# The rounded half of the first 20 weight splits, moved from GpSimd to ScalarE

## Chip, cores and metric

The kernel runs on one core of one Trainium2 chip. The metric is the device time of one execution in microseconds (us). A core has five engines with a queue each, and every queue is worked off in its written order: TensorE (PE in the profile, PEld its weight loads), VectorE (DVE), ScalarE (ACT), GpSimd (POOL) and SyncE (SP), which issues all the transfers. Engines wait for each other by semaphores only.

## What is computed

The reference puts a batch of 8 sequences of 256 tokens with 512 features (2048 tokens) through four layers, each with weights of its own and conditioned on a vector per sequence:

```python
x = _L0_cond_ref(x, pos_BxS, cond_2048, ...)   # norm, attention (8 heads, rope), gated MLP 512-2048-512
x = _L1_cond_ref(x, cond_2048, ...)            # norm, attention (16 heads, unit q and k), MLP with gelu
x = _L2_cond_ref(x, cond_2048, ...)            # norm, attention with a latent k/v and a sparse mask
x = _L3_cond_ref(x, cond_2048, ...)            # experts (64-256-64), norm, silu, projection
```

All of it is float32. A product with a weight is made from split operands: a number is the sum of its rounded half (hi, in the type fp32r, which TensorE reads fast) and the difference (lo), and the kernel adds the products hi*hi, hi*lo and lo*hi.

## The kernel before

The 2048 tokens are four blocks `n` of 512 tokens. The work is planned as one list of steps (`plan.steps`): each chain of steps (a norm, a projection, a head's softmax) has its places in a table of numbers, and the list is sorted by them. `Weights.spread` puts the handling of weights between those steps. Every engine's function then walks through this one list and takes out of it what is its own, so the order on each engine is that of the list. An engine that waits at one step holds back all its later steps.

A weight piece has 128 x 512 numbers. There are 119 that are split. A piece goes three ways, in steps of the list:

- `load`: SyncE brings the piece into one of two staging buffers, `ST`. The load of piece i waits for the end of the split of piece i - 2, since they share a buffer.
- `split`: GpSimd makes the rounded half (a `tensor_scalar`, here called hi-i, L375 in the profile) and then the difference (a `tensor_tensor`, here lo-i, L378), both into one of the eight slots of `W`. The rounded half waits for the load, for the last reader of what stood in the slot (`left`, a matmul on TensorE) and for the store of it (`written`).
- `store`: SyncE writes both halves to `kept` in DRAM; a later use of the piece is a `fetch` from there.

The pieces are numbered here by `weights.order`. Pieces 0 to 4 belong to the first projections (q and k/v), 5 to 8 are the output weights `o` of layer 0, 9 to 16 and 21 on are those of its MLP (`gate` and `up`), 17 to 20 are `down`.

Around the change, ScalarE has these steps: `nsqr` (squares of x, T<-X), `nhi` (rounded half of a normalized tile, HA<-FB or HM<-FB), `raw` and `kvraw` (a projection's result out of PSUM, FB<-B), `exp` (SS<-B), `copy` of the turned probabilities (PT<-B), `cx` (CX<-B) and `act` (FB<-B). The step `cond` is two small activations, each behind a load of an activation table. VectorE has `nfin` (the normalized tile, FB<-X), `nlo` (the difference that goes with `nhi`, HA<-FB,HA) and `nsq` (the sums of the squares, T<-T). TensorE's steps that matter are `out` (CX times `o`, 12 matmuls for each of four tiles), `nvar` (few,T) and `up` (HM,W). The bank in PSUM that `out` number 2 writes is freed by `exp` 18.

In the list the splits of pieces 0 to 4 stand ahead of the first `nhi`. Around the outputs of block 0 the list reads, with what is on other engines left out:

```
out 0, split 13, out 1, split 14, exp 18, out 2, out 3, split 15, split 16, exp 19, cond, copy 16, nsqr
```

(In this line `split 13` to `split 16` are the pieces by `weights.order`.) The slot of piece 13 holds the weights that `out 0` reads, that of piece 14 those of `out 1`, and so on.

Of the kernel before, what the change touches and what calls it, by code (L numbers as in the profile page):

```python
# [10 lines left out]
ACT = mybir.ActivationFunctionType  # L11
ALU = mybir.AluOpType
# [10 lines left out]
PIECES = 123  # L23
WSLOTS = 8
STAGES = 2
FBUFS = 7
VBUFS = 3
AHEAD = 2
# [937 lines left out]
def program(nc, xT, pos, condT, biasd, cols, consts, tab2, wpack, adaw, out):  # L966
    ctx = ExitStack()
    with ctx:
# [3 lines left out]
        def tally(name, step=1):  # L972
            return Tally(ctx.enter_context(nc.semaphore(name)), step)

        X = sb("X", [128, 4, TOK])
        W = sb("W", [128, WSLOTS, 2, 512], F32R)
        ST = sb("ST", [128, STAGES, 512])
# [40 lines left out]
        def col(name, i=0):  # L1018
# [4 lines left out]
        weights = Weights(plan.steps)  # L1023
# [4 lines left out]
        s_st = [tally(f"s_st{k}", 16) for k in range(STAGES)]  # L1028
# [11 lines left out]
        a_sq, a_aff, a_nhi = tally("a_sq"), tally("a_aff"), tally("a_nhi")  # L1040
        a_sin, a_cos, a_raw, a_qsq, a_wide = (tally(x) for x in ("a_sin", "a_cos", "a_raw", "a_qsq", "a_wide"))
        a_v, a_vraw, a_ck, a_exp, a_pt, a_cx = (tally(x) for x in ("a_v", "a_vraw", "a_ck", "a_exp", "a_pt", "a_cx"))
        a_act, a_ghi = tally("a_act"), tally("a_ghi")
        a_gelu, a_y = tally("a_gelu"), tally("a_y")
# [9 lines left out]
        d_tg, d_xl = tally("d_tg"), tally("d_xl")  # L1054

        g_const, g_whi, g_wlo, g_rstd = (tally(x) for x in ("g_const", "g_whi", "g_wlo", "g_rstd"))
        g_cos, g_qlo, g_qr, g_norm, g_xb = (tally(x) for x in ("g_cos", "g_qlo", "g_qr", "g_norm", "g_xb"))

        tallies = [
            s_const, *s_x0, s_x, s_pos, s_tab, s_out, *s_st, s_ad, s_cv, s_ct, s_id, s_rot, s_swap, p_adt, d_ad, *s_w, p_ada, p_tot, p_var, p_bc, p_qkv, p_rot, p_ss,  # L1060
            p_nb, p_sc, p_tr, p_va, p_out, p_up, p_down, p_first, p_second, p_last, a_silu, a_sm, a_sq,
            a_aff, a_nhi, a_sin, a_cos, a_raw, a_qsq, a_wide, a_v, a_vraw, a_ck, a_exp, a_pt, a_cx, a_act, a_ghi, a_gelu,
            a_y, d_ada, d_sm, d_gb, d_sum, d_sub, d_sq, d_var, d_nmul, d_nlo, d_trig,
            d_swap, d_sin, d_qk, d_qhi, d_khi, d_klo, d_qmax, d_ck, d_max, d_neg, d_rec, d_pt, d_cx, d_xo, d_gate, d_glo,
            d_xd, d_tg, d_xl, g_const, g_whi, g_wlo, g_rstd, g_cos, g_qlo, g_qr, g_norm, g_xb]
# [95 lines left out]
        def left(w):  # L1161

            y = weights.before[w]
            tl, key = wused[y] if y >= 0 else (p_ada, (-1,))
            return tl.of(*key)

        def written(w):

            return s_w[weights.slot(w)].of("store", weights.before[w])
# [582 lines left out]
        def scalar(e):  # L1752
# [4 lines left out]
            for step in weights.steps:  # L1757
                kind, a = step[0], step[1:]
                if kind == "cond":
                    e.wait_ge(*s_ct.of())  # L1760
                    e.activation(CT[:, 1, :, :], CT[:, 0, :, :], ACT.Silu).then_inc(*a_silu.up())
                    e.wait_ge(*d_sm.of())
                    e.activation(SM[:, :], SM[:, :], ACT.Exp).then_inc(*a_sm.up())
                elif kind == "nsqr":
                    i, half = a
                    for c in (2 * half, 2 * half + 1):
# [9 lines left out]
                elif kind == "nhi":  # L1776
                    i, c, f = a
                    scale_j, shift_j = affine(i)
                    n, x, hi = i[2], fr.buf(f), target(i, c)[0]
# [29 lines left out]
                elif kind == "kdc":  # L1809
                    n, u = a  # L1810
                    e.wait_ge(*p_qkv.of("kd", 2, n, 0))
                    w = number(n, *LATENT)
# [42 lines left out]
                elif kind == "vc":  # L1855
# [3 lines left out]
                    for j in range(2 if L == 1 else 1):  # L1859
# [3 lines left out]
                        if L == 1:  # L1863
                            o, src = o[:, 2 * half:2 * half + 2, :], dp.buf(u)[:, :].rearrange("p (m d) -> p m d", m=2)
                            src = src[:, :, 128 * j:128 * j + 128]
                        else:
                            vc = 64 if L == 0 else 128
                            o, src = o[:, :, 0:vc], dp.buf(u)[:, 0:4 * vc].rearrange("p (m d) -> p m d", m=4)
# [3 lines left out]
                elif kind == "exp":  # L1872
                    g, us, su, nu = a
                    L, w, nh = layer(g), keys(g), HEADS[layer(g)]
                    nm, s = nmr.buf(nu), ssr.buf(su)
# [64 lines left out]
        def gpsimd(e):  # L1940
            for step in weights.steps:
                kind, a = step[0], step[1:]
# [5 lines left out]
                elif kind == "split":  # L1948
# [2 lines left out]
                    src = ST[:, i % STAGES, :]  # L1951
                    hi, lo = W[:, s, 0, :], W[:, s, 1, :]
                    e.wait_ge(*s_st[i % STAGES].of(w))
                    e.wait_ge(*left(w))
                    e.wait_ge(*written(w))
                    e.tensor_scalar(hi, src, 1.0, 0.0, ALU.mult, ALU.add).then_inc(*g_whi.up(w))
                    e.wait_ge(*g_whi.of(w))
                    e.tensor_tensor(lo, src, hi.bitcast(F32), ALU.subtract).then_inc(*g_wlo.up(w))
                    stused[i] = (g_wlo, (w,))
                elif kind == "nrs":  # L1960
# [259 lines left out]
```

## Time and profile before

| | before |
|---|---|
| median of 3 runs | 1900.38 us (1898.62 to 1901.28) |
| the profiled execution | 1895.2 us, its span 1893.4 us, mean granted clock 0.99 |
| TensorE busy | 1834.1 us, 97% of the span |
| VectorE busy | 1116.1 us, 59% |
| ScalarE busy | 1042.3 us, 55% |
| GpSimd busy | 820.9 us, 43% |

Busy shares are means over the whole span. The first 200 us look otherwise than the rest: TensorE has gaps there and GpSimd is busy for more than half of the time. All 20 pieces of the change are split in the first 145 us.

### The profile page before, as it was taken

The page shows a single profiled execution, that of the slowest core. Times are in us where ns is not written, and L with a number is a line of the kernel's source. Part 1 is how long each engine was busy: PE and PEld are TensorE (multiplying, and loading weights), DVE is VectorE, ACT ScalarE, POOL GpSimd, SP SyncE. Part 2 cuts the span into 40 slices and gives each one's busy share as a digit, 9 for nine tenths or more (in the row PEclk, how much of TensorE's full clock was granted, in tenths as well). Part 3 has the DMA queues.
Part 4 walks back from the last instruction along what each step waited for, and adds up shares of the span by engine and source line. Part 5 has one row for each costly group of instructions (what it writes and reads, how often), then busy time and mean ns, then how long its engine had stood idle before and what let it go on. Part 6 is the DMA issues. An engine that isn't in the chain of part 4 may idle for free.

```text
span 1893.4 us, 35293 instructions
## 1 busy us (share of the span) xinstructions
PE 1834.1 (97%) x12840; PEld 1477.2 (78%) x12840; DVE 1116.1 (59%) x3224; ACT 1042.3 (55%) x2501; POOL 820.9 (43%) x1094
## 2 busy tenths in 40 slices
PE   5899999999999999999999999999999999989988
PEld 3678888888888888888788888888886878865666
DVE  5867445643553356534775488577455786576563
ACT  3654432543343445554465566467468765559975
POOL 5767671211213244333677565335452443244320
PEclk9999999999999999999999999999999999999988
DMA  6436787555545543445356544533532453522422
GB/s 240 150 124 233 266 280 270 181 210 185 182 163 176 190 171 137 173 168 185 132 177 236 170 149 140 193 125 124 194 120 89 149 197 129 185 100 91 139 68 62
DMA packets 98652, 314.77 MB, mean 166 GB/s; under 512 B 11568, under 2 KB 13232, under 8 KB 96944
## 3 DMA queue, kind: packets, MB, share of 16 engines
q1 hardware_dynamic: 98480, 312.52, 47.8%
q8 instruction: 103, 1.69, 0.4%
q14 instruction: 69, 0.57, 0.1%
HBM read 242.48 MB, written 66.58 MB: 163 GB/s over the span
## 4 chain that ended last, share of the span: by engine, by line
PE 87%; DVE 4%; ACT 3%; POOL 3%; DMA 2%; issue 1%; SPq 0%; DVEq 0%; POOLq 0%; ACTq 0%
PE B L360 79%; PE B L363 7%; POOL W L378 1%; DVE T L378 1%; DVE FB L381 1%; POOL SS L375 1%; DMA ST<-in_wpack 1%; ACT SS L366 1%; ACT L366 1%; POOL W L375 0%; DVE SS L384 0%; POOL FB L378 0%; DMA W<-kept 0%; DVE Y L378 0%; DMA Y<-in_adaw 0%
## 5 line engine op out<-in xcount | busy, mean ns | idle before, releaser
L360 PE MATMUL B<-HM,W 128*128 128x512 f32 x2304 | 537.2, 391 | 1.7 <-DVE HM L381 1.2
L375 POOL TENSOR_SCALAR SS<-SS,NM 128x256 f32<-128x256 f32 (+1 forms) x640 | 302.7, 490 | 523.0 <-DVE NM L390 520.6
L360 PEld LDWEIGHTS B<-HM,W 128*128 128x128 f32 x2304 | 429.8, 188 | 93.8 <-DVE HM L381 2.6
L360 PE MATMUL B<-G,W 128*128 128x512 f32 x1536 | 377.5, 396 | 0.0
L360 PEld LDWEIGHTS B<-G,W 128*128 128x128 f32 x1536 | 282.1, 188 | 60.9 <-issue 2.6
L366 ACT ACTIVATE SS<-SS,NM 128x256 f32<-128x256 f32 (+1 forms) x512 | 239.9, 472 | 44.9 <-DVE NM L384 44.3
L360 PE MATMUL B<-HA,W 128*128 128x512 f32 x864 | 218.8, 403 | 6.9 <-DVE HA L378 4.6
L378 POOL TENSOR_TENSOR R<-R,few 128x16 f32<-128x16 f32 (+2 forms) x57 | 121.3, 2130 | 178.2 <-DVE R L375 178.1
L360 PEld LDWEIGHTS B<-HA,W 128*128 128x128 f32 x864 | 160.3, 191 | 46.2 <-issue 4.7
L366 ACT ACTIVATE FB<-B 128x512 f32<-128x512 f32 (+2 forms) x148 | 86.2, 594 | 173.0 <-PE B L360 167.3
L363 PE MATMUL B<-ident,SS 128*128 128x128 f32 x1152 | 164.7, 280 | 9.3 <-POOL SS L375 5.0
L366 ACT ACT_TABLE_LOAD x126 | 161.7, 1283 | 18.8 <-DVE NM L375 11.1
L378 POOL TENSOR_TENSOR W<-ST,W 128x512 fp32r<-128x512 f32 x119 | 161.0, 1353 | 9.9
L363 PEld LDWEIGHTS B<-ident,SS 128*128 128x128 f32 x1152 | 134.2, 144 | 38.9 <-issue 12.8
L366 ACT ACTIVATE PT<-B 128x512 f32<-128x512 f32 x160 | 93.7, 590 | 91.1 <-PE B L363 90.5
L375 POOL TENSOR_SCALAR W<-ST 128x512 fp32r<-128x512 f32 x119 | 78.9, 663 | 149.4 <-PE B L360 102.0
L378 DVE TENSOR_TENSOR G<-FB,G 128x512 fp32r<-128x512 f32 x128 | 100.4, 797 | 70.2 <-ACT G L366 69.7
L360 PE MATMUL B<-CX,W 128*128 128x512 f32 (+1 forms) x624 | 138.6, 376 | 0.6 <-ACT SS L366 0.5
L378 DVE TENSOR_TENSOR FB<-FB,B 128x512 f32<-128x512 f32 x64 | 43.8, 685 | 158.6 <-PE B L360 146.4
L360 PEld LDWEIGHTS B<-CX,W 128*128 128x128 f32 x624 | 109.9, 188 | 22.7 <-issue 2.7
L366 ACT ACTIVATE G<-FB 128x512 fp32r<-128x512 f32 x128 | 79.3, 629 | 83.6 <-DVE FB L378 76.3
L372 DVE COPY PT<-B 128x512 f32<-128x512 f32 x128 | 87.4, 683 | 60.7 <-PE B L363 60.5
(111 smaller groups left out, 2615.0 us busy)
## 6 DMA issues: line engine op xcount, KB each, us to landing
W<-kept SPq DMA_DIRECT2D x357, 512.0 KB, 4.3
kept<-W SPq DMA_DIRECT2D x119, 512.0 KB, 4.6
ST<-in_wpack SPq DMA_DIRECT2D x139, 256.0 KB, 2.9
Y<-in_adaw SPq DMA_DIRECT2D x12, 1024.0 KB, 7.1
FB<-FB SPq DMA_DIRECT2D x52, 64.0 KB, 3.0
X<-in_xT SPq DMA_DIRECT2D x1, 3072.0 KB, 12.8
out_xT<-X SPq DMA_DIRECT2D x12, 256.0 KB, 4.3
FB<-in_pos SPq DMA_DIRECT2D x4, 256.0 KB, 5.3
```

The lines of the kernel that those rows point to most:

```text
L360: return self.real.matmul(*a, **k) if self.real is not None else self
L363: return self.real.transpose(*a, **k) if self.real is not None else self
L366: return self.real.activation(*a, **k) if self.real is not None else self
L372: return self.real.tensor_copy(*a, **k) if self.real is not None else self
L375: return self.real.tensor_scalar(*a, **k) if self.real is not None else self
L378: return self.real.tensor_tensor(*a, **k) if self.real is not None else self
L381: return self.real.scalar_tensor_tensor(*a, **k) if self.real is not None else self
```

## The change

For pieces 0 to 19 ScalarE makes the rounded half, with an activation of the kind Copy, and counts it in a new semaphore `a_whi`. It takes over the waits for the load, for the slot's last reader and for the store. GpSimd waits for `a_whi` and makes the difference only. From piece 20 on nothing changes.

```diff
@@ -23,6 +23,7 @@
 STAGES = 2
+FIRST_SPLITS = 20
 FBUFS = 7
@@ -1761,6 +1763,13 @@
                     e.activation(SM[:, :], SM[:, :], ACT.Exp).then_inc(*a_sm.up())
+                elif kind == "split" and weights.order[a[0]] < FIRST_SPLITS:
+                    w, = a
+                    s, i = weights.slot(w), weights.order[w]
+                    e.wait_ge(*s_st[i % STAGES].of(w))
+                    e.wait_ge(*left(w))
+                    e.wait_ge(*written(w))
+                    e.activation(W[:, s, 0, :], ST[:, i % STAGES, :], ACT.Copy).then_inc(*a_whi.up(w))
                 elif kind == "nsqr":
@@ -1951,10 +1960,13 @@
                     e.wait_ge(*s_st[i % STAGES].of(w))
-                    e.wait_ge(*left(w))
-                    e.wait_ge(*written(w))
-                    e.tensor_scalar(hi, src, 1.0, 0.0, ALU.mult, ALU.add).then_inc(*g_whi.up(w))
-                    e.wait_ge(*g_whi.of(w))
+                    if i < FIRST_SPLITS:
+                        e.wait_ge(*a_whi.of(w))
+                    else:
+                        e.wait_ge(*left(w))
+                        e.wait_ge(*written(w))
+                        e.tensor_scalar(hi, src, 1.0, 0.0, ALU.mult, ALU.add).then_inc(*g_whi.up(w))
+                        e.wait_ge(*g_whi.of(w))
                     e.tensor_tensor(lo, src, hi.bitcast(F32), ALU.subtract).then_inc(*g_wlo.up(w))
```

ScalarE at the start of the program before the change, from the squares of the first block (T<-X) to the first projection's result (FB<-B):

```order
3 L366 ACTIVATE T<-X 128x512 x4
4 L366 ACTIVATE HA<-FB 128x512 x4
5 L366 ACT_TABLE_LOAD
6 L366 ACTIVATE TR<-FB,CV 128x512 x2
7 L366 ACTIVATE FB<-B 128x512
```

The same place with the change:

```order
3 L367 ACTIVATE T<-X 128x512 x4
4 L367 ACTIVATE W<-ST 128x512 x5
5 L367 ACTIVATE HA<-FB 128x512 x4
6 L367 ACT_TABLE_LOAD
7 L367 ACTIVATE TR<-FB,CV 128x512 x2
```

Five rounded halves now stand between the squares and the four `nhi` of the first norm.

ScalarE around the outputs of block 0 before the change. SS,NM<-B,NM are `exp`, two instructions each, CX<-B is `cx`, and the two table loads with CT and SM are `cond`:

```order
57 L366 ACTIVATE SS,NM<-B,NM 128x256 x4
58 L366 ACTIVATE CX<-B 128x256
59 L366 ACTIVATE SS,NM<-B,NM 128x256 x4
60 L366 ACT_TABLE_LOAD
61 L366 ACTIVATE CT<-CT 128x128
62 L366 ACT_TABLE_LOAD
63 L366 ACTIVATE SM<-SM 128x4
64 L366 ACTIVATE PT<-B 128x512
65 L366 ACTIVATE T<-X 128x512 x4
```

The same place with the change:

```order
64 L367 ACTIVATE SS,NM<-B,NM 128x256 x4
65 L367 ACTIVATE W<-ST 128x512
66 L367 ACTIVATE CX<-B 128x256
67 L367 ACTIVATE W<-ST 128x512 x2
68 L367 ACTIVATE SS,NM<-B,NM 128x256 x2
69 L367 ACTIVATE W<-ST 128x512 x2
70 L367 ACTIVATE SS,NM<-B,NM 128x256 x2
71 L367 ACT_TABLE_LOAD
72 L367 ACTIVATE CT<-CT 128x128
73 L367 ACT_TABLE_LOAD
74 L367 ACTIVATE SM<-SM 128x4
75 L367 ACTIVATE PT<-B 128x512
```

The rounded halves of pieces 13 and 14 now stand ahead of `exp` 18, and those of 15 and 16 ahead of `exp` 19 and all that follows it. No table load is added anywhere in ScalarE's order.

GpSimd at the start before the change, the small power of the first norm and the first splits:

```order
9 L378 TENSOR_TENSOR R<-R,few 128x4
10 L375 TENSOR_SCALAR W<-ST 128x512
11 L378 TENSOR_TENSOR W<-ST,W 128x512
12 L375 TENSOR_SCALAR W<-ST 128x512
13 L378 TENSOR_TENSOR W<-ST,W 128x512
```

The same place with the change:

```order
9 L379 TENSOR_TENSOR R<-R,few 128x4
10 L379 TENSOR_TENSOR W<-ST,W 128x512 x5
11 L379 TENSOR_TENSOR FB<-FB,TR 128x512 x2
12 L379 TENSOR_TENSOR Q<-FB,Q 128x512
```

The differences keep their places, and the rounded halves ahead of them are gone.

## Rows read from the trace of the kernel before

**Rows 1.** The page, part 1: busy time, share and instructions of each engine.
```profile
PE 1834.1 (97%) x12840; PEld 1477.2 (78%) x12840; DVE 1116.1 (59%) x3224; ACT 1042.3 (55%) x2501; POOL 820.9 (43%) x1094
```
**Rows 2.** Chain that ended last, 30 to 130 us: start us, us, what.
```profile
49.11 0.60 POOL W L375
...
61.95 0.82 POOL W L375
...
93.21 0.70 POOL W L375
...
115.41 0.60 POOL W L375
```
**Rows 3.** Tile W on GpSimd: ns min/median/max, first and last start, forms.
```profile
L375 POOL TENSOR_SCALAR W<-ST x119: 612/619/1062, 12.7 to 1516.0; 128x512 fp32r<-128x512 f32 x119
L378 POOL TENSOR_TENSOR W<-ST,W x119: 1260/1291/1803, 13.8 to 1516.7; 128x512 fp32r<-128x512 f32 x119
```
**Rows 4.** The page, part 5: a ScalarE rounding of the same shape.
```profile
L366 ACT ACTIVATE G<-FB 128x512 fp32r<-128x512 f32 x128 | 79.3, 629 | 83.6 <-DVE FB L378 76.3
```
**Rows 5.** DMA issues at 4.9 to 5.6 us: KB each, us to landing.
```profile
ST<-in_wpack SPq DMA_DIRECT2D x2, 256.0 KB, 7.4
```
**Rows 6.** The page, part 6: issues of the whole run, median us to landing.
```profile
W<-kept SPq DMA_DIRECT2D x357, 512.0 KB, 4.3
...
ST<-in_wpack SPq DMA_DIRECT2D x139, 256.0 KB, 2.9
```
**Rows 7.** Timeline of ScalarE, the first nhi: start us, us, [idle before, releaser].
```profile
18.10 0.63 ACT L366 ACTIVATE HA<-FB 128x512 fp32r<-128x512 f32 x1 [10.10 <-DVE FB L381]
```
**Rows 8.** Timeline of VectorE, first and last nlo of the first norm.
```profile
18.77 1.63 DVE L378 TENSOR_TENSOR HA<-FB,HA 128x512 fp32r<-128x512 f32 x1
...
23.50 2.36 DVE L378 TENSOR_TENSOR HA<-FB,HA 128x512 fp32r<-128x512 f32 x2
```
**Rows 9.** Groups by form on VectorE, 16.5 to 26 us: count, busy us, mean ns.
```profile
L378 DVE TENSOR_TENSOR HA<-FB,HA 128x512 fp32r<-128x512 f32 x4 | 5.6, 1395 | 0.1
```
**Rows 10.** The same groups, 126.5 to 131 us.
```profile
L378 DVE TENSOR_TENSOR HM<-FB,HM 128x512 fp32r<-128x512 f32 x4 | 2.7, 686 | 0.1
```
**Rows 11.** Timeline of TensorE, 96 to 135 us: outputs 2 with 3, and nvar.
```profile
109.33 5.73 PE L360 MATMUL B<-CX,W 128*128 128x512 f32 x24 [0.54 <-ACT SS L366]
...
120.90 1.71 PE L360 MATMUL B<-few,T 128*128 128x1 f32 x8
```
**Rows 12.** Timeline of ScalarE: exp 18, exp 19, the squares of x.
```profile
108.17 0.48 ACT L366 ACTIVATE SS<-B,NM 128x256 f32<-128x256 f32 x1 [6.11 <-DVE NM L375]
...
109.08 0.47 ACT L366 ACTIVATE SS<-B,NM 128x256 f32<-128x256 f32 x1
...
115.82 2.19 ACT L366 ACTIVATE T<-X 128x512 f32<-128x512 f32 x4 [1.95 <-DVE X L378]
```
**Rows 13.** Timeline of GpSimd: rounded halves of pieces 14 and 16.
```profile
108.95 0.62 POOL L375 TENSOR_SCALAR W<-ST 128x512 fp32r<-128x512 f32 x1 [0.90 <-issue]
...
115.37 0.63 POOL L375 TENSOR_SCALAR W<-ST 128x512 fp32r<-128x512 f32 x1
```
**Rows 14.** Timeline of VectorE: the sums of the squares.
```profile
117.00 3.37 DVE L378 TENSOR_TENSOR T<-T 128x512 f32<-128x512 f32 x3 [0.62 <-ACT T L366]
```
**Rows 15.** Timeline of GpSimd: rounded half of piece 17.
```profile
136.58 0.62 POOL L375 TENSOR_SCALAR W<-ST 128x512 fp32r<-128x512 f32 x1
```
**Rows 16.** Timeline of ScalarE: the first two act of the MLP.
```profile
140.04 1.09 ACT L366 ACTIVATE FB<-B 128x512 f32<-128x512 f32 x2
```
**Rows 17.** Timeline of SyncE: the fetch for the q projection.
```profile
146.97 0.36 SPq L396 DMA_DIRECT2D W<-kept  x1
```
**Rows 18.** Timeline of TensorE: that projection.
```profile
155.07 2.99 PE L360 MATMUL B<-HA,W 128*128 128x512 f32 x12
```
**Rows 19.** Busy time of PE, PEld, DVE, ACT, POOL by windows; then PEclk, DMA, GB/s.
```profile
16.00:20.00 4.00, 0.48 (x1) 0.18 (x1) 3.43 (x10) 1.26 (x2) 3.09 (x4) 1.00 0.54 148
...
120.00:124.00 4.00, 3.59 (x19) 3.19 (x17) 3.10 (x12) 2.23 (x7) 2.05 (x4) 0.50 0.91 307
```

More of the change, by code:

```diff
@@ L1056, in program @@
         g_const, g_whi, g_wlo, g_rstd = (tally(x) for x in ("g_const", "g_whi", "g_wlo", "g_rstd"))
+        a_whi = tally("a_whi")
         g_cos, g_qlo, g_qr, g_norm, g_xb = (tally(x) for x in ("g_cos", "g_qlo", "g_qr", "g_norm", "g_xb"))
@@ L1061, in program @@
             p_nb, p_sc, p_tr, p_va, p_out, p_up, p_down, p_first, p_second, p_last, a_silu, a_sm, a_sq,
-            a_aff, a_nhi, a_sin, a_cos, a_raw, a_qsq, a_wide, a_v, a_vraw, a_ck, a_exp, a_pt, a_cx, a_act, a_ghi, a_gelu,
+            a_whi, a_aff, a_nhi, a_sin, a_cos, a_raw, a_qsq, a_wide, a_v, a_vraw, a_ck, a_exp, a_pt, a_cx, a_act, a_ghi, a_gelu,
             a_y, d_ada, d_sm, d_gb, d_sum, d_sub, d_sq, d_var, d_nmul, d_nlo, d_trig,
```

## The prediction

> **What bounds the kernel now.** I read the busy shares first: TensorE works for 97% of the span [rows 1], so after the first 200 us there is next to nothing to win or to lose but TensorE's own work, and what the start loses stays lost. I then read the chain that ended last in the first 130 us, since the 20 pieces lie there. GpSimd's rounded halves are links of it at four places only, with 0.60, 0.82, 0.70 and 0.60 us [rows 2]. Last I read ScalarE's, GpSimd's, VectorE's and TensorE's timelines at each of the 20 places, asking of every rounded half what it waits for and what now stands behind it.
>
> **Upper bound of the gain.** GpSimd is rid of 20 instructions of 0.62 us (the median) [rows 3], 12.4 us. Only what stood on the chain can shorten it: 0.60 + 0.82 + 0.70 + 0.60 = 2.7 us. The rest GpSimd had spent while others were late.
>
> **The cost in work.** A rounding of this shape takes ScalarE 0.63 us [rows 4], so 12.6 us of work go to an engine that is busy for 55% [rows 1]. That alone would mostly be hidden in its waits. What counts is that ScalarE also takes over the waits.
>
> **Term 1, the start.** The load of piece i waits for the difference of piece i - 2, and five rounded halves now stand ahead of the first nhi. The first two loads are issued from about 5.0 us on and land 7.4 us later [rows 5], so they are there at about 12.4 us, some 0.3 us ahead of GpSimd's first rounding at 12.7 [rows 3]. From there, with 0.63 for a rounded half, 1.29 for a difference [rows 3] and 2.9 for a load [rows 6]: hi-0 until 13.0, lo-0 until 14.3, load 2 until 17.2, hi-2 until 17.9, lo-2 until 19.2, load 4 until 22.1, hi-4 until 22.8. Pieces 1 and 3 run in the gaps. The first nhi had started at 18.10 and had waited for VectorE's tile alone [rows 7]. It now starts at 22.8 and ends at 23.4, and the first nlo starts then in place of 18.77 [rows 8].
>
> Not all of these 4.7 us are lost. From the start of the first nlo to the end of the last VectorE took 23.50 + 2.36 - 18.77 = 7.1 us [rows 8], with the differences at a mean of 1.395 us [rows 9], while GpSimd was splitting. The same four take 0.686 us in the next norm, where GpSimd rests [rows 10]. That is 4 x 0.71 = 2.8 us of stretching, of which only the first difference (beside lo-4) should keep its share: 7.1 - 2.8 + 0.7 = 5.0 us. The last nlo then ends at 28.4 in place of 25.86: **+2.5 us**. Bounds: +1.8 with no stretching left, +4.6 with all of it. TensorE's first products need all four differences and it has nothing else to do there, so all of it shows.
>
> **Term 2, the middle (pieces 5 to 12).** Here the rounded half stands directly ahead of a raw or kvraw that waits for the very matmuls that free the slot, so ScalarE does not wait longer, and each costs 0.63 us [rows 4] which mostly falls into ScalarE's next wait. What GpSimd gains is cut down by its waiting for ScalarE, which comes to piece 7 only behind a raw. Of the first three links [rows 2] I count the first as lost and the other two at half, 0.76 us, and against them one rounding of 0.63 us at a place where ScalarE is waited for (the kvraw behind piece 10 is the likeliest): **-0.1 us**. Bounds: -2.1 with the three links whole and +1.3 with two roundings in full and no gain.
>
> **Term 3, the outputs of block 0.** hi-14 needs the slot that output 1 reads, and GpSimd, idle ahead of it, could start it at 108.95 [rows 13]. On ScalarE it runs from then to 109.6, ahead of exp 18, which began at 108.17 [rows 12]. That is +1.4 us for exp 18, and output 2 starts when exp 18 has freed its bank: the row of TensorE names this releaser [rows 11]. Outputs 2 and 3 thus end at 109.33 + 5.73 + 1.4 = 116.5. hi-16 needs the end of output 3 (115.1 before, and GpSimd's came at 115.37 [rows 13]) and now runs until 117.1. Behind it stands exp 19, begun at 109.08 before [rows 12]: 8 us late. From exp 19 to the squares ScalarE has a fixed stretch of two exp, two table loads and a copy: it had been ready for the squares at 115.82 - 1.95 = 113.87, so the stretch is 113.87 - 109.08 = 4.8 us. The squares start at 121.9 in place of 115.82: the 1.95 us of waiting for VectorE's x are used up, and 6.1 us remain. They take 2.19 us and end at 124.1; the last of the three sums ends 0.7 us later, at 124.8, in place of 117.00 + 3.37 = 120.4 [rows 14]. (The three sums had been stretched to 1.12 us each beside GpSimd's work, and now wait for the squares instead.) nvar on TensorE, 120.90 before [rows 11], is **4.4 us** late. Nothing on TensorE fills this: in its order the values of the pair 16 stand ahead of nvar, and they wait for the copy on ScalarE, which is as late. Bounds: +3.5 (the sums fully behind the squares, one gap less) and +6.0 (the sums stretched as before).
>
> **Term 4, pieces 17 to 19.** GpSimd rounded piece 17 at 136.58 [rows 15]. ScalarE comes to it after the first act, 140.04 + 0.6 [rows 16] (both on the clock of before), so lo-17 and the chain of loads behind it slip by 4.1 us. The nearest user that I find is the fetch for the q projection: issued at 146.97 [rows 17], it would go out at about 151.1 and land 4.3 us later [rows 6], 155.4, for matmuls at 155.07 [rows 18]. **+0.2 us**; bounds 0 and +2.
>
> **Sum.** 2.5 - 0.1 + 4.4 + 0.2 = +7.0 us. The profiled execution took 1895.2 us and would take 1902.2. It is 5.2 us below the median of the runs, so against the median, 1900.38, I say 1907.4 us, in round numbers 1907. A loss here is not given back later: the next wait in the chain, GpSimd's for a slot behind `down`, is for TensorE itself, and TensorE then has no gaps.
>
> **The clock.** TensorE was at half of its 2.4 GHz, 0.50, in 120 to 124 us [rows 19], behind the outputs, where it waits for others. With the change its waiting there grows by 4.4 us, and at the start by 2.5. The 24 matmuls of outputs 2 and 3 take 5.73 us at the full clock, 0.24 each [rows 11]; 15 of them at half clock would cost 3.6 us more. I leave that out of the sum, since at the start TensorE worked for 0.48 us out of 4 and its clock stayed at 1.00 [rows 19].
>
> The Trainium skill, "TensorE: Matmul & The Clock Gate", section "What's actually happening", has the clock halved after an idle stretch and restored after a busy one. By that rule the longer gap at the start halves it as well, and the sum would be 7.0 + 3.6 = 10.6 us; the trace agrees at 120 us and does not at the start. This is part of the rival "heavier".
>
> **The rivals.**
> 1. *Forecast*, ScalarE's queue is held back at the start and at the outputs: +3.8 to +10 us. For it: both waits are forced by the order and have rows. Chance 0.60.
> 2. *Covered*: ScalarE comes to the splits at better times than I worked out, or the released VectorE and GpSimd give back more (the whole 2.7 us of rows 2, all of the stretching). With the low bounds, 1.8 - 2.1 + 3.5 + 0 = +3.2 us, 1903.6, within 0.2%. Against it: the order puts exp 19 behind output 3 whatever the durations. Chance 0.22.
> 3. *Heavier*: the clock drops at the start (+3.6), and VectorE's differences stay stretched (+2.1 over term 1): 7.0 + 5.7 = +12.7 us, 1913. Chance 0.10.
> 4. *Faster*: the place is the same stretch of the outputs, and the mechanism is that the copies of this stretch are not what TensorE waits for. If the values and nvar had more than 4.4 us of slack, term 3 would fall away, and with the stretching gone at the start and the links of rows 2 won: 1.8 - 2.7 = -0.9 us, 1899.5; only a further 3 us, from all VectorE work of the 145 us running less stretched, would make it over 0.2% faster. It decides from some 8 us of such gains on. Against it: TensorE waits in rows 11 for exp 18 by name. Chance 0.08.
>
> **How the numbers follow.** A change of this kernel can be told from none from about 0.2% on, 3.8 us. Faster 0.08, within it 0.22, slower 0.60 + 0.10 = 0.70. The range leaves out about a tenth on each side: from +0.6 us, 1901, inside the covered case, to +13 us, 1913.5, the heavier one. The forecast's own range is 1904 to 1910.5.
>
> **What would show it.** In the profile after: ScalarE's five W<-ST between 12.4 and 22.8 with waits for ST loads, the first HA<-FB at 22 to 23.5, the last HA<-FB,HA near 28; one W<-ST near 109 ahead of exp 18, two around 114 and 116.5, T<-X at about 6 us after its place of before (plus what the start has shifted), and nvar some 3 us further behind the end of output 3 than now. TensorE's work stays as it is; its idle time in the first 160 us grows by 6 to 7 us. The prediction is wrong if the first nhi starts before 21, if exp 19 stands less than 5 us behind its place relative to output 1, or if TensorE has other work in the gap.

## The result

| | before | after |
|---|---|---|
| median | 1900.74 us (4 runs, 1898.62 to 1901.28) | 1909.88 us (4 runs, 1909.36 to 1914.04) |
| the profiled execution | 1895.2 us, span 1893.4 us | 1909.36 us, span 1907.5 us, mean clock 0.988 |

The ratio is 1.0059, 95% interval 1.0045 to 1.0073, or 11.2 us of 1900 (8.6 to 13.9); the two medians as such are 9.1 us apart. The change makes the kernel slower. The profiled execution of before lies 5.5 us below its median, that of after 0.5 us below its own, so the two spans are 14.1 us apart, 5 us more than the medians.

**The work moved as planned.** The page after, part 1, answers to [rows 1]; ScalarE got 20 instructions more and GpSimd 20 fewer:

```profile
PE 1834.9 (96%) x12840; PEld 1479.7 (78%) x12840; DVE 1114.2 (58%) x3224; ACT 1053.4 (55%) x2521; POOL 807.0 (42%) x1074
```

Tile W on ScalarE after (ns min/median/max, first and last start; then its idle time ahead of these, in us and times, by releaser):

```profile
L367 ACT ACTIVATE W<-ST x20: 615/629/637, 12.1 to 157.0; 128x512 fp32r<-128x512 f32 x20
...
  PE B L361: 17.2, 9
  DMA ST<-in_wpack: 12.8, 5
  issue: 8.7, 3
```

This is the first thing to see. The 20 rounded halves are 12.6 us of work on ScalarE, and ScalarE stood idle ahead of them for 17.2 + 12.8 + 8.7 = 38.7 us. Most of that isn't new waiting: up to the q projection ScalarE was idle for 77.8 us before and for 81.9 after. It waits at other places. Before, it waited for what it was to do next; now it waits at roundings, and whatever stands behind them in its queue is held back, ready or not. GpSimd had waited little at its splits (5.1 us ahead of all its writes of W in the first 146 us). Now it waits for ScalarE ahead of 15 of the differences, 23.1 us.

**The places.** ScalarE's timeline after (start us, us, [idle before, releaser]); it answers to [rows 7, 12, 16]:

```profile
17.12 0.63 ACT L367 ACTIVATE W<-ST 128x512 fp32r<-128x512 f32 x1 [3.79 <-DMA ST<-in_wpack]
...
22.19 0.63 ACT L367 ACTIVATE W<-ST 128x512 fp32r<-128x512 f32 x1 [2.92 <-DMA ST<-in_wpack]
22.73 1.13 ACT L367 ACTIVATE HA<-FB 128x512 fp32r<-128x512 f32 x2
...
115.50 0.63 ACT L367 ACTIVATE W<-ST 128x512 fp32r<-128x512 f32 x1 [2.55 <-PE B L361]
116.04 0.46 ACT L367 ACTIVATE SS<-B,NM 128x256 f32<-128x256 f32 x1
...
120.26 0.63 ACT L367 ACTIVATE W<-ST 128x512 fp32r<-128x512 f32 x1 [3.21 <-issue]
122.98 0.63 ACT L367 ACTIVATE W<-ST 128x512 fp32r<-128x512 f32 x1 [2.09 <-PE B L361]
123.52 0.46 ACT L367 ACTIVATE SS<-B,NM 128x256 f32<-128x256 f32 x1
...
128.05 2.18 ACT L367 ACTIVATE T<-X 128x512 f32<-128x512 f32 x4
```

At the start hi-2, hi-3 and hi-4 wait for their loads and the first nhi starts at 22.73, where it had started at 18.10. At the outputs hi-14 stands at 115.50 ahead of exp 18, hi-15 and hi-16 at 120.26 and 122.98, and exp 19 begins at 123.52.

VectorE's timeline after, which answers to [rows 8, 14]: the first and last nlo, and the sums of the squares.

```profile
23.37 1.41 DVE L379 TENSOR_TENSOR HA<-FB,HA 128x512 fp32r<-128x512 f32 x1 [4.52 <-ACT HA L367]
...
26.87 1.47 DVE L379 TENSOR_TENSOR HA<-FB,HA 128x512 fp32r<-128x512 f32 x2
...
129.22 2.28 DVE L379 TENSOR_TENSOR T<-T 128x512 f32<-128x512 f32 x3 [4.99 <-ACT T L367]
```

The four differences took 23.37 to 28.34, 5.0 us, where they had taken 7.1 beside GpSimd's splits. TensorE's timeline after, which answers to [rows 11, 18], and SyncE's fetch, which answers to [rows 17]:

```profile
24.93 7.59 PE L361 MATMUL B<-HA,W 128*128 128x512 f32 x24 [8.30 <-DVE HA L379]
32.35 1.02 PE L361 MATMUL B<-FB,rotm 128*128 128x512 f32 x2
...
117.19 5.71 PE L361 MATMUL B<-CX,W 128*128 128x512 f32 x24 [1.77 <-ACT SS L367]
...
128.29 1.98 PE L361 MATMUL B<-PT,V 128*64 128x128 f32 x16 [4.96 <-ACT PT L367]
...
132.69 1.49 PE L361 MATMUL B<-few,T 128*128 128x1 f32 x7
...
169.91 3.02 PE L361 MATMUL B<-HA,W 128*128 128x512 f32 x12 [2.80 <-DMA W<-kept]
```

```profile
163.04 0.36 SPq L397 DMA_DIRECT2D W<-kept  x1
```

I laid TensorE's milestones of both traces side by side. How far after is behind before at each:

| milestone | before | after | behind by |
|---|---|---|---|
| first rotation | 30.35 | 32.35 | 2.0 |
| output 0 of block 0 | 102.62 | 109.25 | 6.6 |
| output 2 | 109.33 | 117.19 | 7.9 |
| nvar | 120.90 | 132.69 | 11.8 |
| q projection | 155.07 | 169.91 | 14.8 |
| end of the span | 1893.4 | 1907.5 | 14.1 |

Three of these steps were forecast as places of loss: the start (+2.0), the outputs (+5.2 from output 0 to nvar) and, for next to nothing, the q projection (+3.0). The 4.6 us between the first rotation and output 0 weren't forecast. TensorE has the same 465 matmuls in this stretch in both traces and is busy with them for 59.83 us before and for 62.69 after, so 2.9 of the 4.6 us are slower matmuls and not waiting. The windows after (us, busy time of PE, PEld, DVE, ACT, POOL, then granted clock, DMA share and GB/s) show TensorE at a lower clock in 44 to 48 us, a window in which before had 1.00:

```profile
24.00:28.00 4.00, 3.08 (x7) 2.06 (x8) 3.91 (x8) 1.63 (x3) 0.23 (x1) 1.00 0.95 355
44.00:48.00 4.00, 3.57 (x24) 2.83 (x21) 2.72 (x7) 1.82 (x7) 2.84 (x5) 0.72 0.96 389
...
128.00:132.00 4.00, 3.71 (x29) 3.19 (x30) 2.19 (x5) 2.61 (x6) 0.33 (x1) 0.50 0.78 257
132.00:136.00 4.00, 3.60 (x17) 3.20 (x17) 2.75 (x10) 2.45 (x8) 1.94 (x4) 0.50 0.00 0
```

Whether those 4.6 us belong to the change, no trace by itself can say. The experiments had to.

### The profile page after: what moved, and what is told of

Its sections match the earlier page's. It is cut to its first block, busy times and chain, and to the rows that moved or that the text cites. A ratio compares the mean times of both kernels' runs of the same rounds, so it can differ in the third digit from the quotient of the medians.

```text
span 1907.5 us, 35307 instructions
## 1 busy us (share of the span) xinstructions
PE 1834.9 (96%) x12840; PEld 1479.7 (78%) x12840; DVE 1114.2 (58%) x3224; ACT 1053.4 (55%) x2521; POOL 807.0 (42%) x1074
## 4 chain that ended last, share of the span: by engine, by line
PE 84%; DVE 4%; ACT 2%; DMA 2%; POOL 1%; issue 1%; SPq 0%; DVEq 0%; POOLq 0%; ACTq 0%
PE B L361 76%; PE B L364 7%; DMA ST<-in_wpack 1%; DVE FB L382 1%; POOL W L379 1%; DVE T L379 1%; ACT L367 1%; ACT SS L367 0%; ACT GF L367 0%; DVE SS L385 0%; DMA Y<-in_adaw 0%; DMA W<-kept 0%; DVE Y L379 0%; DVE HM L382 0%; POOL W L376 0%
## 5 line engine op out<-in xcount | busy, mean ns | idle before, releaser
L379 POOL TENSOR_TENSOR W<-ST,W 128x512 fp32r<-128x512 f32 x119 | 159.6, 1341 | 31.5 <-ACT W L367 23.1
L376 POOL TENSOR_SCALAR W<-ST 128x512 fp32r<-128x512 f32 x99 | 64.6, 652 | 144.9 <-PE B L361 101.2
```

The costliest lines, as they stand in the source:

```text
L376: return self.real.tensor_scalar(*a, **k) if self.real is not None else self
L379: return self.real.tensor_tensor(*a, **k) if self.real is not None else self
```

## The experiments

All ran in three sets, each beside the kernel before on the same chip, whose medians were 1899.8, 1900.1 and 1899.0 us over 31 to 34 runs. The kernels of a set had 9 or 11 runs each. Their intervals are about 0.001 wide to each side, or 1.9 us. The us in this text are the ratio times 1900. Each set ran on a chip of its own, so a difference between kernels of two sets goes by way of before and is less certain.

### One part of the change at a time

Four kernels make only some of the rounded halves on ScalarE. The edit to the kernel after is one list, with `range(0, 5)`, `range(5, 13)`, `range(13, 17)` and `range(17, 20)`:

```diff
-FIRST_SPLITS = 20
+ON_SCALAR = range(0, 5)
...
-                elif kind == "split" and weights.order[a[0]] < FIRST_SPLITS:
+                elif kind == "split" and weights.order[a[0]] in ON_SCALAR:
...
-                    if i < FIRST_SPLITS:
+                    if i in ON_SCALAR:
```

> Only pieces 0 to 4 are rounded on ScalarE. If the held-back first nhi costs what the two traces show (the first rotation on TensorE 2.0 us later), this kernel is 2 us (0.1%) slower than before. If the loss at the start is given back within the next 50 us, by TensorE's gaps there, it is the same within 0.5 us. If only half of the stretching of VectorE had gone, as in the pessimistic bound, it would be 4.6 us.

> Only pieces 5 to 12 are rounded on ScalarE. In the profile of the changed kernel TensorE falls back by another 4.6 us between the first rotation and the outputs of block 0, where I had forecast -0.1. Theory 1: it is ScalarE's queue in these places (rounding ahead of raw and kvraw, GpSimd waiting for it), then 3 to 4.6 us slower. Theory 2: it is TensorE's clock, which the profile shows at half in 44 to 50, 80 to 84 and 100 to 104 us, and that comes from the shift at the start; then this kernel is within 1 us of before. Rival: a gain of up to 2.1 us from the three links of the chain.

> Only pieces 13 to 16. By the forecast's own chain of steps +4.4 us, by the two traces +5.2 us (0.27%), with exp 18 1.2 us and exp 19 about 7 us behind its place of before. If the roundings' work and not their waits were the cause, 4 x 0.63 = 2.5 us at most.

> Only pieces 17 to 19. The forecast had +0.2 us. The two traces show TensorE waiting 2.8 us for the fetch of a q piece. If that wait belongs to these three pieces alone, +2.8 to 3 us; if it needs the earlier shifts too (loads and stores already late), 0 to 0.5 us.

| pieces on ScalarE | ratio to before (95% interval) | us | forecast term |
|---|---|---|---|
| 0 to 4 | 1.0012 (1.0002 to 1.0023) | +2.3 | +2.5 |
| 5 to 12 | 1.0000 (0.9991 to 1.0010) | 0.0 | -0.1 |
| 13 to 16 | 1.0024 (1.0013 to 1.0035) | +4.6 | +4.4 |
| 17 to 19 | 1.0022 (1.0012 to 1.0033) | +4.2 | +0.2 |
| sum of the four | 1.0058 | +11.1 | +7.0 |
| all 20, the change | 1.0059 (1.0045 to 1.0073) | +11.2 | |

The parts add up to the whole. Each has an interval of about 2 us to each side and the sum one of about 4, so an interplay of a few us isn't excluded. Pieces 5 to 12 cost nothing that can be measured, and by their interval 1.9 us at most: the 4.6 us that the trace after lost between the rotation and output 0 are not, or not mainly, their price. Three terms agree with the forecast, and the fourth was too small by 4 us (2.1 to 6.1).

### Only the work, without the waits

The kernel before, with a 128x512 copy of a constant on ScalarE at each of the 20 places; nobody reads its result. GpSimd splits as before. (`a_idle` counts the copies; the list of counters and one later wait for it are left out here.)

```diff
+                elif kind == "split" and weights.order[a[0]] < 20:
+                    i = weights.order[a[0]]
+                    if i >= 4:
+                        e.wait_ge(*a_idle.of(i - 4))
+                    e.activation(GF[:, i % 4, :], few[:, 0:1].broadcast_to([128, 512]), ACT.Copy).then_inc(*a_idle.up(i))
```

> The kernel before, with GpSimd rounding as it did, and an added copy of 128 x 512 on ScalarE at each of the 20 places where the changed kernel has a rounding. The copies read a constant, write to a buffer that is not yet in use, and wait for nobody but the copy four places earlier. This is the work of the change without its waits. If the waits make the loss, this kernel is the same as before, within 1 us. If ScalarE's work did it, up to 11 us slower, and 2 to 3 us at the least.

It took 0.9998 of before (0.9989 to 1.0007). The same number of instructions of the same size in the same places costs nothing that can be measured. So it is waiting that costs. This kernel doesn't say whose: in it ScalarE doesn't wait for loads and slots, and GpSimd doesn't wait for ScalarE either. The kernels below show both.

### The outputs: pieces 15 and 16 alone

The list is `(15, 16)`.

> Only pieces 15 and 16 are rounded on ScalarE, ahead of exp 19 and behind exp 18. By the forecast's chain exp 19 now waits for the end of output 3 without outputs 2 and 3 being later themselves: exp 19 6.7 us late, the squares 4.7 us, nvar 3 us late, so 3 to 4 us of the 4.6 that all four pieces cost, and 1.3 for pieces 13 and 14. Rival: outputs 2 and 3 being held by exp 18 is the main part; then 1 us or less here.

1.0022 (1.0012 to 1.0031), +4.2 us of the 4.6 of this part. ScalarE's timeline of this kernel:

```profile
109.70 0.48 ACT L367 ACTIVATE SS<-B,NM 128x256 f32<-128x256 f32 x1 [6.11 <-DVE NM L376]
...
116.68 0.63 ACT L367 ACTIVATE W<-ST 128x512 fp32r<-128x512 f32 x1 [2.09 <-PE B L361]
117.22 0.46 ACT L367 ACTIVATE SS<-B,NM 128x256 f32<-128x256 f32 x1
```

Exp 18 (109.70) is as early as before relative to the outputs, and exp 19 (117.22) still stands 7.5 us behind it, where before had 0.9 [rows 12]. Most of the term hangs on the one line: hi-16, which waits for the end of output 3, ahead of exp 19. How much is left for pieces 13 and 14 the times can't tell, since 0.4 us is far inside the intervals. The traces say 1.2 us: from output 0 to nvar it is 18.28 us before, 22.23 in this kernel and 23.42 with all four pieces, that is +4.0 and +5.1, close to the split that was expected.

### The outputs: the same four pieces, other places

Pieces 13 to 16 on ScalarE, with hi-14 behind exp 18, and hi-15 and hi-16 behind the squares. Only ScalarE's own walk through the list is changed; GpSimd keeps its order.

```diff
...
+            at = steps.index(next(y for y in steps if y[0] == "exp" and y[1] == 19))
+            last = [y for y in steps[at:] if y[0] == "nsqr"][1]
+            for i, behind in [(14, ("exp", 18)), (16, last), (15, last)]:
+                x = next(x for x in steps if x[0] == "split" and weights.order[x[1]] == i)
+                steps.remove(x)
+                steps.insert(next(k for k, y in enumerate(steps) if y[:len(behind)] == behind) + 1, x)
```

> Pieces 13 to 16 on ScalarE, but its rounded half of piece 14 stands behind exp 18, and those of 15 and 16 behind the squares of the norm that follows. My theory, that exp 18, exp 19 and the squares held back are the loss: it falls from 4.6 us to -0.5 to +1.2 us, nvar as before. The rival, that the later splits of 15 and 16 now make the loads of 17 and 18 late, or that GpSimd's later differences stretch the norm: +2 to +4 us stay.

My theory missed: 1.0030 (1.0019 to 1.0040), +5.7 us, no less than the 4.6 of the unmoved kernel. ScalarE, GpSimd and TensorE in the trace of this kernel, one timeline each:

```profile
114.90 2.19 ACT L367 ACTIVATE T<-X 128x512 f32<-128x512 f32 x4 [1.48 <-DVE X L379]
116.99 1.14 ACT L367 ACTIVATE W<-ST 128x512 fp32r<-128x512 f32 x2
```

```profile
117.75 1.73 POOL L379 TENSOR_TENSOR W<-ST,W 128x512 fp32r<-128x512 f32 x1 [7.43 <-ACT W L367]
...
120.36 1.26 POOL L379 TENSOR_TENSOR W<-ST,W 128x512 fp32r<-128x512 f32 x1
121.58 1.26 POOL L379 TENSOR_TENSOR Q<-FB,Q 128x512 fp32r<-128x512 f32 x1
```

```profile
122.90 1.65 PE L361 MATMUL B<-KB,Q 64*128 64x256 f32 x12 [6.72 <-POOL Q L379]
```

ScalarE is free of the wait: the squares start at 114.90, even a little earlier than in [rows 12]. But now GpSimd stands idle for 7.43 us at lo-15, because hi-15 comes so late, and behind lo-16 in its queue is the q tile (Q<-FB,Q) that TensorE needs. It waits 6.72 us for it; before it had waited 1.98. From output 0 to nvar it is 23.40 us, as in the unmoved kernel. The cost didn't go away, it moved from one queue to the other. Between exp 18 and that q tile there may be no place for the two roundings that suits both. A kernel in which GpSimd's two differences move as well, behind the q tile, was not tried.

### The start: what stretches, and what waits

Three kernels. In the first (of the kernel before) GpSimd waits for the last nlo before it splits piece 2, so that VectorE has the four differences to itself:

```diff
+                    if i == 2:
+                        e.wait_ge(*d_nlo.of(("a", 0, 0), 3))
```

> The kernel before, where GpSimd starts the split of piece 2 only when VectorE has made the last difference of the first norm. Nothing is on ScalarE. If GpSimd's splits stretch VectorE's differences there (a mean of 1.395 us against 0.686), the last one ends 2.8 us earlier and the kernel is up to 2.8 us faster; with the pieces' loads, stores and fetches up to 5 us later, if one of these is needed in time, nothing or a loss.

```profile
27.29 1.02 PE L360 MATMUL B<-FB,rotm 128*128 128x512 f32 x2
...
36.85 1.02 PE L360 MATMUL B<-KB,Q 64*128 64x256 f32 x12 [3.04 <-DVE KB L381]
```

TensorE's timeline above: the first rotation is 3.06 us earlier than before. The time is 0.9996 (0.9987 to 1.0005), the same. At the first scores (KB,Q), 36.85 against 37.71, 2.2 of the 3.06 us are gone, and at the first sums (few) it is at 66.06 against 66.17. GpSimd's timeline of this kernel names the reason for the first part:

```profile
29.22 1.26 POOL L378 TENSOR_TENSOR W<-ST,W 128x512 fp32r<-128x512 f32 x1
30.44 2.52 POOL L378 TENSOR_TENSOR FB<-FB,TR 128x512 f32<-128x512 f32 x2
```

The two rope products (FB<-FB,TR) on the way to the first scores stand behind lo-4, which was put off with the other splits. How much of the 3.06 us is the edit's doing is less sure: with an untouched start the first rotation came anywhere from 27.90 to 31.76 us in seven traces (last section). What the edit surely did is to free VectorE: its four differences took 0.69 us each here, and the last ended at 23.1 us and not at 25.86.

In the second, pieces 0 to 4 are on ScalarE, and hi-2, hi-3 and hi-4 stand behind the last nhi:

```diff
+            late = [x for x in weights.steps if x[0] == "split" and weights.order[x[1]] in (2, 3, 4)]
+            at = weights.steps.index(("nlo", ("a", 0, 0), 2))
+            steps = [x for x in weights.steps[:at] if x not in late] + late + weights.steps[at:]
```

> Only pieces 0 to 4 on ScalarE as in the kernel that lost 2.3 us, but with the roundings of pieces 2 to 4 behind the last nhi in ScalarE's order. No nhi waits for a load now, and GpSimd is quiet during VectorE's differences. If the place in the order made the loss at the start, the loss is gone and the stretching too: 2 us faster than before (bounds 0 and 2.8). If the handing over between the engines costs by itself, still 1 us or more slower.

Missed: 1.0011 (1.0002 to 1.0020), +2.1 us where I had expected a gain. ScalarE and TensorE of this kernel:

```profile
22.37 1.14 ACT L367 ACTIVATE W<-ST 128x512 fp32r<-128x512 f32 x2
28.00 0.63 ACT L367 ACTIVATE W<-ST 128x512 fp32r<-128x512 f32 x1 [4.50 <-DMA ST<-in_wpack]
```

```profile
31.90 3.80 PE L361 MATMUL B<-FB,rotm 128*128 128x512 f32 x4 [4.66 <-ACT FB L367]
```

The load of piece 4 waits for lo-2, which is now later, so hi-4 waits until 28.00, and behind it stand the table load and the copies out of PSUM that the rotation reads.

In the third, hi-2 and hi-3 are behind the last nhi, and hi-4 only behind the first kvraw:

```diff
...
+            for i, behind in [(3, ('nhi', ('a', 0, 0), 3)), (2, ('nhi', ('a', 0, 0), 3)), (4, ('kvraw', ('k', 0, 0, 0)))]:
...
```

> Pieces 0 to 4 on ScalarE again, but its rounded halves of pieces 2 and 3 stand behind the last nhi of the first norm and that of piece 4 behind the first kvraw, so that no wait for a load stands ahead of a step that TensorE waits for. My theory, that the start costs by what is held back behind ScalarE's waits for loads: the first rotation on TensorE begins near 27.3 us, as in the quiet kernel, and the time is that of before, -2 to +0.5 us. The rival, that VectorE's and GpSimd's own stretch or a further wait costs: rotation near 30 or later and still +1 to +3 us.

The time missed again: 1.0012 (1.0004 to 1.0021), +2.3 us. The mechanism at the rotation was right (28.22 in place of 30.35), and then the gain is gone. ScalarE, GpSimd and TensorE of this kernel:

```profile
30.73 0.62 ACT L367 ACTIVATE W<-ST 128x512 fp32r<-128x512 f32 x1
```

```profile
31.49 1.29 POOL L379 TENSOR_TENSOR W<-ST,W 128x512 fp32r<-128x512 f32 x1 [5.14 <-ACT W L367]
32.74 2.52 POOL L379 TENSOR_TENSOR FB<-FB,TR 128x512 f32<-128x512 f32 x2
```

```profile
28.22 1.02 PE L361 MATMUL B<-FB,rotm 128*128 128x512 f32 x2
...
39.15 1.59 PE L361 MATMUL B<-KB,Q 64*128 64x256 f32 x12 [4.42 <-DVE KB L382]
```

It is the outputs' story over again: GpSimd waits 5.14 us for hi-4, and the rope products behind lo-4 come late. TensorE starts the first scores at 39.15 (37.71 before), 1.4 us late, though it was 2.1 us early at the rotation.

### Pieces 17 to 19: the fetch

Pieces 17 to 19 on ScalarE, and SyncE issues the fetch for the q projection ahead of the load that waits for lo-19:

```diff
+            steps.remove(("fetch", 25))
+            steps.insert(steps.index(("split", 23)), ("fetch", 25))
```

> Pieces 17 to 19 on ScalarE, and SyncE issues the fetch of the weights for the q projection ahead of the load that waits for the difference of piece 19, not behind it. If the late fetch is what pieces 17 to 19 cost, the loss falls from 4.2 us to 0 to 1.4 us. The rival, that the loss comes from something else in this stretch (later differences for down, later stores): it stays at 3 to 5 us.

1.0005 (0.9995 to 1.0014), +1.0 us, where the same kernel without the edit had +4.2 on another chip. By the ratios most of the loss is the late fetch. By the medians alone it is less clear, +3.7 without the edit and +2.6 with it. SyncE and TensorE of the kernel without the edit, then of this one:

```profile
152.40 0.36 SPq L397 DMA_DIRECT2D W<-kept  x1
```

```profile
157.79 3.03 PE L361 MATMUL B<-HA,W 128*128 128x512 f32 x12 [1.15 <-DMA W<-kept]
```

```profile
147.78 0.37 SPq L397 DMA_DIRECT2D W<-kept  x1
```

```profile
157.31 3.02 PE L361 MATMUL B<-HA,W 128*128 128x512 f32 x12
```

The fetch goes out 4.6 us earlier and the wait for it is gone. From nvar to the q projection it is 33.9 to 34.2 us in the twelve traces without the late fetch, this kernel among them, 35.60 with pieces 17 to 19 unrepaired and 37.22 in after. So the late fetch costs 1.4 us in the one trace and 3.0 in the other, and the repair takes all of it back. It also travels faster there. The same fetch, by the DMA issues of each trace (KB, us to landing), in before, in after, and in this kernel:

```profile
W<-kept SPq DMA_DIRECT2D x1, 512.0 KB, 5.6
```

```profile
W<-kept SPq DMA_DIRECT2D x1, 512.0 KB, 6.8
```

```profile
W<-kept SPq DMA_DIRECT2D x1, 512.0 KB, 3.4
```

Behind the load and the store it had taken 5.6 us even in before, not the 4.3 of the whole run's median [rows 6]; in after it took 6.8, with the DMA engines busy for 97% from 163 to 170 us. The trace of pieces 17 to 19 alone shows only 1.15 us of waiting and that of the whole change 2.80, while the ratios of the two kernels here are 3.2 us apart. Whether other executions wait as long as the one of after isn't shown. The profiled execution of pieces 17 to 19 was the fastest of its 11.

### All repairs together

All but pieces 15 and 16 on ScalarE, hi-2 to hi-4 placed as in the third kernel of the start, hi-14 behind exp 18, and the early fetch.

> All of pieces 0 to 19 but 15 and 16 on ScalarE, with the start as in the placed kernel of this call, the rounded half of piece 14 behind exp 18, and the early fetch. My theory, that the whole loss of the change is three places where steps were held back: 0 to +1.5 us against before, in place of +11. The rival, that waits of all pieces pile up: +5 us or more.

1.0018 (1.0008 to 1.0029), +3.4 us in place of +11.2, and 2 us above what I expected. It is what the parts sum to: 2.3 for the start, 1.0 for pieces 17 to 19 with the early fetch, and nothing much for the rest. No version with rounded halves on ScalarE was measurably faster than the kernel before.

## Why the prediction was right, and where it was not

The forecast was 1907.0 us, +7.0, with a likeliest range of +3.8 to +10 us. Measured were 1909.9 us, 9.1 above the median of before, and by the ratio +11.2 (8.6 to 13.9). The direction and the mechanism held at the two places that were named. "ScalarE's queue is held back at the start and at the outputs" is what the traces show, and the copies without waits show that the work itself is free. What failed is the size of term 4 and a reading of the clock.

**Term 1, the start** (+2.5; measured +2.3). Step by step: hi-4 until 22.8 (22.82 in the trace), the first nlo 4.7 us late (4.6), the last nlo done at 28.4 (28.34), the first rotation 2.0 us late. The stretching was right as well: 7.1 us fell to 5.0. One premise was wrong. TensorE's first products do not need all four differences; before, it began them behind the first:

```profile
20.55 1.62 PE L360 MATMUL B<-HA,W 128*128 128x512 f32 x3 [3.92 <-DVE HA L378]
```

From the end of the last nlo to the first rotation it was 4.5 us before and 4.0 after, so 0.5 of the 2.5 us didn't reach TensorE.

**Term 2, the middle** (-0.1; measured 0.0, -1.7 to +1.9). Nothing that can be measured, as forecast, though the trace after seemed to say 4.6 us.

**Term 3, the outputs** (+4.4; measured +4.6). Exp 19 was forecast 8 us late relative to the outputs. From output 0 to exp 19 it was 6.5 us before and 14.3 after, 7.8 more. The squares became ready 0.5 us after the copy and no longer waited for x, and nvar came 5.2 us late relative to output 0, for 4.4. The sums of the squares were unstretched, 2.28 us for 3.37, as the term assumed. The share of hi-14, 1.4 us for exp 18, showed in the trace (1.77 us of waiting ahead of output 2 in place of 0.54), and the kernel with pieces 15 and 16 alone, whose nvar is 1.2 us less late, agrees.

**Term 4, pieces 17 to 19** (+0.2, bounds 0 and +2; measured +4.2, 2.3 to 6.3). This is the step that failed, by its size: "it would go out at about 151.1 and land 4.3 us later, 155.4, for matmuls at 155.07". The transfer, the queue and the slip were right: after runs 11.8 us behind at nvar, and the fetch, 146.97 before and 163.04 after, is 16.1 behind, so it slipped by 4.3 us against TensorE, for 4.1 forecast. The flight was wrong. I had taken the median of 357 fetches, 4.3 us [rows 6]; this one took 5.6 in before already and 6.8 in after, and its matmuls started 6.87 us after its issue. With 5.6 for 4.3 the term is about +1.6, against 1.4 in the trace of pieces 17 to 19 alone. With 6.8 it is 0.2 + 2.5 = +2.7, against 3.0 in the trace after (14.8 - 11.8) and 3.2 us between the ratios of the two kernels that differ in the fetch alone. What makes up the rest of the 4.2 us stays open; 1.0 us of it stayed with the early fetch, within that kernel's interval of nothing.

**The clock.** "I leave that out of the sum, since at the start ... its clock stayed at 1.00" misreads the start. The column of the granted clock says 1.00 there, 24 to 28 us after included. But the products of the first norm ran at half pace. Here are the matmuls of 128x512 in 24 to 26 us, first before, then in the kernel with the copies, whose granted clock in that window is 0.50, and last before in 28 to 30 us (count: ns min/median/max, first and last start):

```profile
L360 PE MATMUL B<-HA,W x6: 628/628/792, 23.4 to 25.9; 128*128 128x512 f32 x6
```

```profile
L360 PE MATMUL B<-HA,W x6: 628/628/762, 23.5 to 26.0; 128*128 128x512 f32 x6
```

```profile
L360 PE MATMUL B<-HA,W x10: 387/396/411, 27.8 to 29.9; 128*128 128x512 f32 x10
```

The trace of before holds no record of the clock ahead of 27.8 us, that of after none ahead of 28.7, and the view shows 1.00 where it has none. These products begin at about 628 ns each in all fourteen traces and turn to about 390 somewhere from 23 to 30 us. In before 13 of the 24 took over 600 ns, in after 8. So the clock was down at the start with and without the change, and the longer gap of 8.30 us lost nothing more by it. That 3.6 us were left out of term 1 was right, but not for the reason given; nor has its "15 of them" a row. By the rule of the Trainium skill, "TensorE: Matmul & The Clock Gate", section "What's actually happening", an idle stretch halves the clock. Read by the matmuls' durations, this trace agrees with it at the start, with 628 ns behind 8.30 us of waiting (what the clock was ahead of that wait is not on record), as it does behind the outputs, where after 4.96 us of waiting the granted clock was 0.50, half of 2.4 GHz, in 128 to 136 us.

Of term 3 the clock is a part. The kernel with pieces 13 to 16 was below 1.00 for four windows of 4 us from 120 us on (0.59, 0.50, 0.50, 0.70), before for two (0.50, 0.65). From output 0 to nvar TensorE had the same 89 matmuls before and after and was busy with them for 15.40 us and 16.71 us: about 1.3 of the 5.2 us are slower matmuls, which the sum had left out, and 3.9 are waiting. TensorE's idle time up to the q projection grew by 12.1 us, from 32.1 to 44.2, where the prediction had 6 to 7.

**The range** (1901 to 1913.5). The median, 1909.9, lies in the forecast's own range of 1904 to 1910.5; the +11.2 of the ratio lies above it, and the full range takes that in only because the rival "heavier" had stretched it to the top. Neither the further clock loss at the start nor the stretching of "heavier" came, so that part is luck: I hadn't seen where the missing 4 us were.

## What to carry to other kernels

A step that is moved to another engine takes its waits with it, and in a queue that is worked off in order the waits are the price: 12.6 us of added work alone cost nothing, and the same instructions with their waits cost 11 us. It isn't the sum of the waiting that counts (ScalarE's idle time grew by 4 us) but what stands behind each wait. List for each moved instruction what it waits for and what stands behind it, on its new engine, on the engine that now waits for its result, and on the DMA queue whose transfers it releases; and take the flight of such a transfer from its own row, not from the median of its kind (5.6 and 6.8 us for 4.3 here). When one wait is placed better, look at the other queue before you expect a gain: at both places here the loss only changed sides.

## What the runs showed of the hardware that I had not expected

**Ahead of its first record the clock column says nothing.** At the start of eleven of the fourteen traces the granted clock is given as 1.00 while the matmuls of 128x512 take 628 ns, as they do in the other three, which have 0.50 on record there; at full clock they take 389. The durations of equal matmuls are the check.

**The same start takes different times.** Up to the first rotation the kernels before, with pieces 5 to 12, 13 to 16, 15 and 16, 17 to 19, the one with moved outputs and the one with the early fetch do the same, and it begins at 30.35, 29.95, 31.24, 31.20, 30.79, 27.90 and 31.76 us. Output 0, up to which six of the seven do the same, comes from 101.99 to 104.67. After that start comes a fall of the granted clock whose place I can't tie to a kernel: below 1.00 in 52 to 60 us in before, 44 to 52 in after and in the kernel with pieces 0 to 4, 40 to 52 with pieces 5 to 12. Behind the outputs every trace has one, somewhere between 116 and 136 us. So a milestone of one trace against one other is uncertain by 2 to 3 us within the first 105 us, the 2.0 us at the first rotation among them. Of the 4.6 us of after between the rotation and output 0, 2.9 are slower matmuls. The trace with pieces 5 to 12 also has this stretch longer, 75.57 us, where the five others with the same start as before, and before itself, have 72.27 to 74.09, but the times of that kernel show no loss. Whether those pieces have a part in it is open.

**Of VectorE and GpSimd the one that came second was stretched.** Differences of 128x512 took 1.395 us each on VectorE beside GpSimd's splits [rows 9] and 0.69 us where GpSimd rested. Which of the two engines was slowed changed with 0.2 us of their starts. The first nlo and GpSimd's lo-2 (start, ns) in four traces:

| trace | lo-2 on GpSimd | first nlo on VectorE |
|---|---|---|
| before | 18.59, 1260 | 18.77, 1630 |
| pieces 17 to 19 | 18.74, 1270 | 18.92, 1640 |
| pieces 5 to 12 | 19.16, 1590 | 18.84, 780 |
| outputs moved | 18.86, 1820 | 18.85, 680 |

In six of the eight traces in which GpSimd makes the first splits as before it came first, and VectorE took 1.63 to 1.77 us; in the two others VectorE came first, and GpSimd was the slow one. In these two the last nlo ended at about 24.2 us, where it was 25.8 in before. That is one source of the spread above.
